# A new table rule and step order, and the replicated values of a linear attention laid out key by head

## What is computed

```python
# layer 0: softmax attention, 16 heads of 8; then a ternary FFN with hidden width 512
attn = softmax(einsum('bqd,bkd->bqk', Q, K) / sqrt(8));  ctx = attn @ V;  out = LN(ctx @ wo + bo + x)
h = silu(tlin(x, w1)) * tlin(x, w2);  h = gelu(tlin(h, h1));  h = gelu(tlin(h, h2));  tlin(h, w3)
# layer 1: gated linear attention, 8 heads of 16 keys by 16 values, over 1024 tokens
gk = log_sigmoid(x @ Wgk1 @ Wgk2 + bgk2) / 16
def step(h, inp):
    qt, kt, vt, gt = inp
    h = h * exp(gt)[..., None] + kt[..., None] * vt[..., None, :]
    return h, einsum('bhk,bhkv->bhv', qt, h)
o = o * rsqrt(mean(o * o) + EPS) * g_norm_w * (g * sigmoid(g));  o @ Wo
# layer 1 FFN: 8 zones, the 3 best per batch row by a router
for e in range(N_ZONES): z = gelu(x @ Wa[e]) @ Wb[e];  zone_outputs += z * w[:, e]
```

## Time and profile before

| | |
|---|---|
| median of the runs | 1077.08 us (1076.49 to 1081.83) |
| the profiled execution | 1080.35 us, its span 1078.6 us |
| granted TensorE clock, mean | 0.973 of full speed |
| matmul groups with the most time | L1485 294.0 us, L1448 189.2 us, L1517 183.5 us |
| the exponentials, L914 | 486.8 us |
| the scans, L1261 | 192.5 us |
| data moved by DMA | 106.27 MB, 99 GB/s over the span |

### The profile page before, as it was taken

How to read it: one execution, slowest core, us unless ns; L and a number is a source line. 1 busy time by engine, 2 the same in 40 slices (tenths; PEclk the granted TensorE clock), 3 DMA queues, 4 the chain that set the end, 5 groups by cost and what they waited for, 6 DMA issues and landing times.

```text
span 1078.6 us, 16699 instructions
## 1 busy us (share of the span) xinstructions
PE 978.0 (91%) x5842; PEld 462.2 (43%) x5842; DVE 707.4 (66%) x1267; ACT 846.4 (78%) x1082; POOL 343.3 (32%) x318
## 2 busy tenths in 40 slices
PE   2998989998898799989989999899889999999998
PEld 1222336222442343334423443354237667655666
DVE  4234652565577556878896696778787888989200
ACT  0998996998797799989999989999977377653542
POOL 1000111112442332434522542334332655646100
PEclk8899999899898899999999999999999999999999
DMA  6755352225504361473136431631332321242020
GB/s 165 183 137 126 96 139 57 76 65 131 129 30 126 90 133 57 108 181 95 45 102 162 116 88 61 180 96 55 104 105 73 98 67 62 91 130 83 11 69 20
DMA packets 139975, 106.27 MB, mean 99 GB/s; under 512 B 91824, under 2 KB 106960, under 8 KB 139856
## 3 DMA queue, kind: packets, MB, share of 16 engines
q1 hardware_dynamic: 134960, 102.77, 35.4%
q10 hardware_dynamic: 4896, 1.87, 0.7%
HBM read 75.25 MB, written 29.36 MB: 97 GB/s over the span
## 4 chain that ended last, share of the span: by engine, by line
PE 51%; ACT 17%; issue 14%; DVE 9%; DMA 5%; POOL 4%; SPq 1%; ACTq 0%; DVEq 0%; POOLq 0%
PE PS L1485 15%; ACT R L914 10%; PE PS L1517 9%; PE PS L1448 9%; PE PS L1632 4%; PE PS L1644 4%; DMA R<-VD 3%; DVE R L1252 3%; PE PS L1557 2%; ACT L881 2%; DVE R L1261 2%; PE PS L1579 2%; POOL R L862 2%; PE PS L1588 1%; PE PS L1383 1%
## 5 line engine op out<-in xcount | busy, mean ns | idle before, releaser
L914 ACT ACTIVATE R<-PS 128x1024 f32<-128x1024 f32 x512 | 486.8, 1038 | 52.7 <-PE PS L1448 50.8
L1485 PE MATMUL PS<-R 128*32 128x512 f32 x2048 | 294.0, 617 | 0.2 <-DVE R L1205 0.2
L862 POOL TENSOR_TENSOR R<-R 128x512 f32<-128x512 f32 x128 | 182.2, 1430 | 175.0 <-ACT R L989 121.6
L1448 PE MATMUL PS<-RA 32*128 32x512 f32 x1024 | 189.2, 506 | 46.4 <-ACT R L914 30.5
L1517 PE MATMUL PS<-RB,WR 128*128 128x512 f32 x640 | 183.5, 430 | 24.6 <-DVE R L1228 10.2
L1261 DVE TENSOR_TENSOR_SCAN R<-R 128x512 f32<-128x512 f32 x128 | 192.5, 1504 | 2.9
L1448 PEld LDWEIGHTS PS<-RA 32*128 32x128 f32 x1024 | 73.7, 185 | 273.2 <-ACT R L914 168.6
L881 ACT ACT_TABLE_LOAD x108 | 138.6, 1283 | 48.7 <-PE PS L1517 23.2
L1517 PEld LDWEIGHTS PS<-RB,WR 128*128 128x128 f32 x640 | 121.1, 196 | 86.8 <-issue 22.4
L1252 DVE TENSOR_TENSOR R<-R 128x512 f32<-128x512 f32 x128 | 108.2, 845 | 28.6 <-DMA R<-VD 28.5
L1038 ACT ACTIVATE R<-PS 128x512 f32<-128x512 f32 x96 | 56.6, 596 | 77.1 <-PE PS L1632 76.6
(11 more groups left out here) (123 smaller groups left out, 844.9 us busy)
## 6 DMA issues: line engine op xcount, KB each, us to landing
R<-VD SPq DMA_DIRECT2D x128, 256.0 KB
RA<-QD SPq DMA_DIRECT2D x64, 256.0 KB, 4.5
QD<-RA SPq DMA_DIRECT2D x56, 256.0 KB, 4.0
RA<-QD SPq DMA_DIRECT2D x64, 128.0 KB, 4.4
OD<-R SPq DMA_DIRECT2D x32, 256.0 KB, 2.1
R<-OD SPq DMA_DIRECT2D x128, 32.0 KB, 2.5
R<-in_Wa SPq DMA_DIRECT2D x12, 256.0 KB, 3.3
R<-in_Wb SPq DMA_DIRECT2D x12, 256.0 KB, 3.9
```

The lines of the kernel that those rows point to most:

```text
L862: pool.tensor_tensor(st, st, Qc, ALU.mult).then_inc(S["qh"], 1)
L914: act.activation(PR[u % 4], bank(2 * s, 1024), ACT.Exp, scale=SC).then_inc(S["exp"], 1)
L1448: op = pe.matmul(bank(2 * s + h), exact(KS[k][p:p + 32, 128 * j:128 * j + 128]), exact(QS[k][p:p + 32, :]), start=True, stop=stop)
L1485: op = pe.matmul(bank(ob)[c:c + 32, :], VAF[b % 2][:, at:at + 32], PR[u % 4][:, 512 * h:512 * h + 512], start=(j == 0), stop=(j == 7), til ...
```

## The change

Three things change together. ScalarE's table rule: exp may use exp_and_others or natural_log_exp_and_others, tanh exp_and_others or either gelu set, ln only natural_log_exp_and_others; where a load is needed, the set is taken that serves the coming functions longest. The string ORDER is another interleaving of the same streams with the same number of letters each. And replica's source pattern has the 16 copies outermost and the 8 heads inside, so that partition p holds head p % 8 and key p // 8 (before: head p // 16, key p % 16); hot, the columns of the weights for queries, keys and decay, and the decay bias follow that layout, on the host.

```diff
-    "xxxxxwxxxxxxqxqxqxxlxxxxxxxxwxxwqxxxxxxxxwxwxxxxxqxxwxxqwxxxfxxxxfxxlxxlxxxxxwxxwxxwxlxwxfxxqfwaxwxx"
...
+    "qxqxqxxxxxxxxxxxxxwxlxxwxwxxqxwxxxxxxxxxxxwxxxxxxqfxxxxxwxxwxxxlxfxwwxxqxxxxlxqxwxxxxwlxxxxpxfxxxwwf"
...
@@ replica @@
-                                                 [[8192, 8], [0, 16], [1, 512]])).then_inc(S["rep_in%d" % (n % 3)], 16)
+                                                 [[0, 16], [8192, 8], [1, 512]])).then_inc(S["rep_in%d" % (n % 3)], 16)
@@ ScalarE @@
-            def tables(name):
-
-                if loaded[0] != name:
-                    loaded[0] = name
-                    act.preload_act_table_set(name)
...
+            EXP, LOG, GELU, APPR = "exp_and_others", "natural_log_exp_and_others", "gelu_and_others", "gelu_apprx_tanh_and_others"
+            sets = {"exp": (EXP, LOG), "ln": (LOG,), "tanh": (EXP, GELU, APPR), "gelu": (GELU,), "appr": (APPR,)}
+            uses = {"scores": ("exp",), "gate": ("tanh",), "gelu": ("gelu",), "decay_1": ("exp", "ln"), "decay_3": ("exp",),
+                    "rms": ("ln", "exp"), "tanh_c": ("tanh",), "route_1": ("tanh",), "route_2": ("exp",), "zone_up": ("appr",)}
+            coming = ["exp"] + [f for step in order for f in uses.get(step[0], ())]
+            state = {"loaded": None, "at": 0}
+
+            def tables(function):
+
+                at = state["at"]
+                assert coming[at] == function
+                state["at"] += 1
+                if state["loaded"] not in sets[function]:
+                    def run(name):
+                        return next((n for n in range(at, len(coming)) if name not in sets[coming[n]]), len(coming))
+                    state["loaded"] = max(sets[function], key=run)
+                    act.preload_act_table_set(state["loaded"])
...
             def scores(u0):
-                log_exp()
+                tables("exp")
...
-                tanh_with("gelu_and_others")
+                tables("tanh")
...
@@ host @@
-            hot[p, j, 8 * j + p // 16] = 1.0
+            hot[p, j, 8 * j + p % 8] = 1.0
...
+    keyed = lanes % 8 * 16 + lanes // 8
...
-        "wC": np.stack([g["L1_attn_Wq"], g["L1_attn_Wk"], g["L1_attn_Wv"], g["L1_attn_Wg"][:, perm],
+        "wC": np.stack([g["L1_attn_Wq"][:, keyed], g["L1_attn_Wk"][:, keyed], g["L1_attn_Wv"], g["L1_attn_Wg"][:, perm],
...
+        "Wgk1": g["L1_attn_Wgk1"].T, "Wgk2": g["L1_attn_Wgk2"][:, keyed], "gsel": gsel,
+        "cC": np.stack([g["L1_attn_bgk2"][keyed], g["L1_attn_g_norm_w"][val]], axis=1), "hot": hot, "bd": bd,
```

More of the change, by code:

```diff
@@ new lines @@
+    "xxlfbfbbxxbxxxqfxxxbxxxxxaaxbxxabxxaxplpxxrrrxpqaqpxpxapqqxfxpxaxxsxxxxbxsxbxsxxsqsxxsxssrxxxssbxqxx"
+    "rxxxlssxbxrssfxbxfbxlxssssbrxxbbrsxxsxxxlxxsxsrxsrsbsxbxbbbfbbxbxssxabssbxssrsrssbsrsbsxxrbbxxsaasxs"
+    "xbxxxsbaxxpssxpsxaxqrsxsrasxxxqssrlxfppxrabqxxxpsxpxsssxspxxxbxsssxxxxxbrqxxrbxbxbxrbxbxbssqsxstxbts"
+    "rbstssxsxbsbsqbbbxxssxxxxrsbststlxrxxfrbllxbbrssxbssxssfsbxsbxxfaxxxxbssrxaaxxrsrxxsxssxxxsrbsxaxpsx"
+    "xpssxxsssxqasxrrxxxxsxsxqxrsprsaqxtxlxtxspxxaxqxpsxbpsxssxspsxxbxxxftqssxbxbrbrrxxbxxxxxqsblsslrxxbb"
@@ new lines @@
+    "sxxlstfsxxsbssxtssbsbsrbxfbbbtxbssxrxbbsxfssbsrsaxbssarssstxbxaxbtxaxtxxxxsbrxxatrxxsxxxtsxsbasrxxsx"
+    "fsssasxtrspxqslxxbpssrxrxrqbqspxqtxxbstbxpsxsqsbxtxxxxsxppttssxsrxxlbxpxssxssxxbxrbsxrrxrsssxxsxslxs"
+    "sxtsssttbxxsfsrlxxtxfxsfsqbbbbbtxbxrbxsxbssxtbsbrxsbssbxxxtarssbxbxaxxasxxasbrraslxxaxrsxxxxsbxsssxs"
+    "qpsxxpsxrxxtxspxsqasxsprxxxbsxsxxrsxrfrssxsqxpxpxsxfqsxsxpxxstbsxxsxsxtxqbrlxbxxbxbrbxsxrbxrlsxlxbtx"
+    "sssxssbssbxfxbbbbbfbssxxxstsxbrxrtxarsssxbssrsbssstsbxbxxbtxxxabxssasxrtrxbxrsssrxsppsxxsxsxxsxxasxx"
@@ new lines @@
+    "xxpxxsstsftsrpaxxxxsssxrxarssxxtsrxapbpsssxsltxpxxxfsbsxsxtrbbbrxxbrxsbrxsbssxtxxsfxbxxtxxtsssbxszbf"
+    "btbbtstsbssbdrbadtbbabassbdazzasbbdatrrsdsddtdsdsrdtddbadbbssssdsdsrbprstdsdbddsdrdbpdsddbdddrzdtsbs"
+    "dszsdsbtsbdsbzdsdpsprtdsdsdrbsssrpbspdssrsdbsbpsbssrbsbddbtrsssdrdddsrdsdssstssdtsbsrttrbsdrssssbdbr"
+    "ssdsdsbddbsttsssdbdrdrssdsbrdrsstsssdppsddpsssdsddprdstrddddtdssstdspdrstrdtddpsstssdsptssrsrdddtdss"
+    "srdsddztsrsssddtsdtssdzstrsssrsdddrddsrtsdsssddtsdsdssrsrszssdrdsrdsddsddsdtdsssdsddsddrssdsdrdssdsd"
@@ L928, in gelu @@
                 need.wait_ge(*ps)
-                tables("gelu_and_others")
+                tables("gelu")
                 act.activation(HL[L][m][:, 1, :], bank(bk), ACT.Gelu, scale=sB[:, scale + m:scale + m + 1]).then_inc(S["gelu"], 1)
@@ L947, in decay_1 @@
                 own.settle()
-                log_exp()
+                tables("exp")
                 own.step(act.activation(G2, G2, ACT.Exp, scale=-1.0))
                 own.settle()
+                tables("ln")
                 act.activation(G2, G2, ACT.Ln, bias=1.0).then_inc(S["g_abs"], 1)
```

29 lines of the change are left out of this document (3 added, 26 removed).

## The result

The changed kernel takes 1042.32 us (1039.06 to 1043.2), the kernel before 1077.63 us beside it: a ratio of 0.966, 95% interval 0.9626 to 0.9694. I had forecast 1059, and the range reached down to 1042, so the result lies at its very edge. The direction was right and the gain, 35 us, was nearly twice what the sum gave. The profiled execution took 1041.97 us.

The account below looks back on a forecast made before the run. TensorE and ScalarE were taken to bound it before 800 us, replica loads and VectorE until 1000. Terms of -8 + 4.5 - 5 - 1.4 - 8 = -18 us took 1080.35 to 1062.4, 1059 for the median (range 1042 to 1079).

Parts of the forecast that it names:

- The split into stages: Attention alone to 165 us, TensorE and ScalarE leading to 800, replica loads and VectorE to 1000, then only zone products.
- ScalarE's share, 37%: 165 to 800 us: ScalarE's part of the chain, used to value 21.8 us of saved table loads at 8 us.
- Part 1, table sets: Table loads fall from 108 to 83: 8 us off before 800 us and 1.4 us off after it.
- Part 2, the order: Ternary FFN work moves ahead of the last scores: 4.5 us added before 800 us, 5 us off after it.
- small waits: Whole kernel: many waits shifted by the new order, not priced one by one, allowed 8 us either way.
- 5 + 1.4 + 8: 800 to 1000 us: savings in us from moved FFN work, fewer table loads and faster replica loads.
- The moved work: Four gate steps and one hidden step of block 6, 24 matmuls, go from behind the scores to before them.
- Part 3, the transfer: Replica loads run on 16 engines instead of 8: 8 us off from 800 to 1000 us, 0 before.
- (a): 800 to 1000 us: the replica transfer is hidden or stays on eight engines, its 8 us go; 1070 us, chance 0.20.
- (c): Replica loads: all engines read one row and queue in memory, landings slow down; 1089 us, chance 0.09.
- (d): Moved FFN work costs 10 us before the scores end, saves 1.8 behind, small waits add 8; 1076 us, chance 0.12.
- (b): Before 800 us ScalarE alone sets the pace, so fewer table loads save 21.8 us, not 8; 1044 us, chance 0.14.

Follow-up runs that it names:

- detour_new: The changed kernel with a load of an unused table set ahead of each of its 83 table loads: 1117.5 us.
- detour_old: The kernel before with a load of an unused table set ahead of each of its 108 table loads: 1196.5 us.
- order_layout: The changed kernel with the old table rule, so 140 table loads instead of 83: 1118.5 us, ratio to before 1.038.
- tables_layout: The kernel before with the new table rule and the new replica layout, but the old order: 1067.1 us, ratio to before 0.991.
- tables_order: The changed kernel with the old replica layout (8 heads outermost): 1048.1 us, ratio to before 0.972.
- layout_only: The kernel before with the new replica layout alone (16 copies outermost): 1068.8 us, ratio to before 0.993.
- tables_only: The kernel before with the new table rule alone, 87 table loads instead of 108: 1075.8 us, ratio to before 0.999.
- no_gelu pair: Tanh in place of gelu in the ternary FFN, once on tables_layout and once on the changed kernel: 1074.7 and 1037.7 us.

## Why the prediction was right and wrong

**What bounds the kernel.** The split into stages held, and the two leaders before 800 us were the right ones. Wrong was to read their shares of the chain as prices. ScalarE's share, 37%, valued 17 loads at 8 us on either order. Measured: nothing for loads taken from the old order (1075.8), 0.71 to 1.04 of their time for loads added (detour_new, detour_old, order_layout), and between 8 us lost and 5 us gained for 60 and 55 us taken off. With ScalarE about 90% busy, TensorE 91 to 94%, and both bound to one sequence, a microsecond of ScalarE had a price for adding and hardly any for taking.

**Part 1, table sets.** The counts were right, 108 and 83. The term of 8 + 1.4 us measured 0.4 us alone and 1.6 beside the layout (1068.8 to 1067.1), neither clear of the spread.

**Part 2, the order.** This is the step that failed: net -0.5 us (+4.5 and -5) with 8 us either way for small waits, where the order is worth 25 us with the new rule. I had put the last exponential some 4 us earlier, and it came 26 us earlier. What stands in the term's place is ScalarE's waits for the FFN's products, 32.9 us of them before and 31.3 in tables_layout, which the new order cut to 11.8. I had rows on these waits and priced none of them; they went under the 8 us for small waits. I also had a clue: 140 loads under the old rule said that the new order does something which the old rule forbids, and I only concluded that it needs the new rule. What it does is to place gate steps singly. That this is the cause of the 25 us is not shown: the gates' own waits were 7.1 us of the 31.3, moving gates alone never gave a part of the gain, and why the waits at the hidden steps fell stays open.

The stretch from the last exponential to the last gather seems to have gone as told, 206 us before and 193 after, 14 less where the terms for it gave 5 + 1.4 + 8. That match is luck. tables_order has 192.3 us there without the layout, so order and rule gave all of it where 6.4 were forecast, and the layout's part lay elsewhere. The moved work was counted a little high too: behind the last exponential the traces have 8 tanh of the gates before and 4 after, but 16 gelus in both, so four gate steps moved and the hidden step did not: 16 matmuls instead of 24.

**Part 3, the transfer.** Right in size and in its mechanism, eight engines to sixteen: 8 us, measured 7.5 alone, 9 beside the new rule, 6 beside rule and order. The place was right on the old order only. I had 8 us behind the last exponential and 0 before it; on the new order it is 0 behind (192.3 and 192.6 us) and the 8.5 us are before it (775.7 and 767.2). The landings on the chain fell to 3.65 and 4.00 us where I had 3.3. VectorE's wait for replicas fell from 28.5 to 20.6 us, not under 15, and 17.6 of these 20.6 stand before the last exponential (18.8 before, 26.1 in tables_order).

**The rivals.** (a), (c) and (d) are out: layout_only is faster by its whole interval, the order does not lose. (b) gave the time, 1044, for a wrong reason: by it the 20 loads less before the last exponential of tables_only would have saved 25.7 us, and they saved nothing; the no_gelu pair says the same.

## What to carry to other kernels

Where two engines share the lead in a fixed sequence, price a removal near nothing and an addition near its full duration (0.71 to 1.04 of it here), until a run says otherwise. Here the freed time paid only with an order made for it, so a rule and its order are to be judged together. If a change ships a new order, add up the waits of each stream that it moves (here 32.9 us for the FFN's products) and take that sum as what the order may win, not a flat allowance. And look at the outermost count of a broadcast load: 8 left half the engines idle here, and swapping two dimensions cost only a permutation on the host.

## What the runs showed of the hardware

A second load of the loaded table set, written right behind the first, isn't in the profile and costs nothing. A load of another set costs 1.283 us by the trace and 0.91 to 1.34 us in the time of the whole kernel, nowhere the 2.66 us that the Trainium skill (ScalarE: Activation LUTs, "What ACT_TABLE_LOAD costs") gives for a switch; had there been a drain of 1.38 us in each, the 108 added loads of detour_old would by an estimate from that figure have taken 288 us of ScalarE; the kernel became 119 us longer, and in detour_new the second load follows the first with 0.4 us of idle time for all 83 together. By the packet counts, a load on the SP queue has one packet more for each engine that takes part: 8 packets more for each load that runs on 16 engines instead of 8 (134960 and 135984 for 128 loads). With ScalarE busy 69 us (detour_new) and 95 us (detour_old) longer up to the last exponential, the granted TensorE clock of that stretch fell from 0.98 to 0.94 (detour_new) and from 0.97 to 0.90 (detour_old).
